# A deformable-convolution block with an expert layer: the bilinear selection weights of one lane group to a PSUM bank, built by 64-by-64 matmuls

## The reference

```python
# x + conv(ln(x)); then t + ffn(ln(t))
x_proj = inputs @ w_in + b_in
x1 = gelu(ln(depthwise3x3(inputs) + dw_bias) * gamma + beta)
offset = (x1 @ w_off + b_off)                # 8 groups x 9 taps x (x, y)
mask = softmax(x1 @ w_mask + b_mask)         # over the 9 taps of a group
px, py = pixel + tap + offset
samp = bilinear_gather(pad(x_proj), px, py)  # 8 channels of each group, 4 corners, zero outside
out = sum over taps(samp * mask) @ w_out + b_out
# ffn: 8 experts of 64 -> 256 (gelu) -> 64, the two best per token, weighted by their softmax
```

## Time and profile before

| | us |
|---|---|
| median of three runs | 310.62 |
| profiled execution | 310.67 |
| its span, first to last instruction | 308.9 |
| PE busy, of the span | 277.8 (90%) |
| ACT busy | 257.3 (83%) |
| DVE busy | 232.1 (75%) |
| POOL busy | 119.7 (39%) |

### The profile page before, as it was taken

How to read it: one execution, slowest core, us unless ns; L and a number is a source line. 1 busy time by engine, 2 the same in 40 slices (tenths; PEclk the granted TensorE clock), 3 DMA queues, 4 the chain that set the end, 5 groups by cost and what they waited for, 6 DMA issues and landing times.

```text
span 308.9 us, 8480 instructions
## 1 busy us (share of the span) xinstructions
PE 277.8 (90%) x3312; PEld 180.1 (58%) x3312; DVE 232.1 (75%) x658; ACT 257.3 (83%) x495; POOL 119.7 (39%) x123
## 2 busy tenths in 40 slices
PE   7977998968799999799999999998979999998895
PEld 2552476635468664345568664444767787676562
DVE  6999769999958859896696879599757244478455
ACT  3788679899797999998797999998868899888463
POOL 5230151504452615032194613050775903549530
PEclk9999999999999999999999999999999999999999
DMA  6920000000000000000000000000000000000000
GB/s 144 299 50 0 3 3 3 1 2 2 0 3 2 3 3 0 2 0 3 2 8 12 2 2 0 3 2 0 2 20 0 3 2 2 11 0 3 11 1 17
DMA packets 7189, 4.84 MB, mean 16 GB/s; under 512 B 5089, under 2 KB 6830, under 8 KB 7086
## 3 DMA queue, kind: packets, MB, share of 16 engines
q1 hardware_dynamic: 7150, 4.31, 5.8%
HBM read 2.04 MB, written 0.52 MB: 8 GB/s over the span
## 4 chain that ended last, share of the span: by engine, by line
PE 44%; ACT 24%; DVE 18%; issue 9%; POOL 4%; DMA 1%; DVEq 0%; ACTq 0%; POOLq 0%
ACT wk L1288 7%; ACT wk L1283 6%; PE m_ps L1653 4%; PE zl_ps L1537 4%; PE ga_ps L1568 3%; PE zh_ps L1534 3%; PE m_ps L1670 3%; PE ga_ps L1570 3%; PE ga_ps L1569 3%; ACT h_all L1319 3%; PE zl_ps L1546 2%; PE zh_ps L1546 2%; DVE prod L870 2%; PE m_ps L1682 2%; PE m_ps L1637 2%
## 5 line engine op out<-in xcount | busy, mean ns | idle before, releaser
L870 DVE TENSOR_TENSOR prod<-ga_ps,wx 128x480 f32<-128x480 f32 x96 | 62.3, 651 | 33.9 <-PE ga_ps L1570 33.6
L1283 ACT ACTIVATE wk<-zh_ps 128x512 f16<-128x512 f32 x108 | 65.2, 604 | 20.2 <-PE zh_ps L1534 19.3
L1568 PE MATMUL ga_ps<-v_all,wk 128*128 128x80 f16 x576 | 79.0, 201 | 3.0 <-DVE prod L870 1.5
L555 POOL TENSOR_TENSOR prod<-prod 128x960 f32<-128x960 f32 (+1 forms) x20 | 37.7, 1885 | 108.4 <-DVE prod L870 108.3
L1570 PE MATMUL ga_ps<-v_all,wk 128*128 128x80 f16 x576 | 79.0, 201 | 0.0
L1569 PE MATMUL ga_ps<-v_all,wk 128*128 128x80 f16 x576 | 79.0, 201 | 0.0
L1568 PEld LDWEIGHTS ga_ps<-v_all,wk 128*128 128x128 f16 x576 | 56.6, 99 | 16.2 <-issue 6.0
L1288 ACT ACTIVATE wk<-zl_ps 128x512 f16<-128x512 f32 x108 | 65.3, 605 | 0.0
L1569 PEld LDWEIGHTS ga_ps<-v_all,wk 128*128 128x128 f16 x576 | 57.1, 99 | 8.5
L1570 PEld LDWEIGHTS ga_ps<-v_all,wk 128*128 128x128 f16 x576 | 57.2, 99 | 0.0
L1537 PE MATMUL zl_ps<-tab,sel_lo 128*128 128x512 f16 x108 | 41.6, 385 | 7.2 <-ACT wk L1288 3.8
(11 more groups left out here) (284 smaller groups left out, 613.8 us busy)
## 6 DMA issues: line engine op xcount, KB each, us to landing
v_all<-still SPq DMA_DIRECT2D x1, 1440.0 KB, 10.2
h_all<-in_W SPq DMA_DIRECT2D x1, 512.0 KB
w_s<-in_W SPq DMA_DIRECT2D x1, 512.0 KB
x_tok<-in_x SPq DMA_DIRECT2D x1, 384.0 KB, 6.6
out_dram<-x_tok SPq DMA_DIRECT2D x6, 64.0 KB, 1.7
w_high<-w_high SPq DMA_DIRECT2D x1, 256.0 KB, 2.9
const<-in_table SPq DMA_DIRECT2D x1, 218.0 KB, 3.1
vec<-in_vectors SPq DMA_DIRECT2D x1, 132.5 KB
```

What stands on the lines that cost most here:

```text
L555: then(pool.tensor_tensor(p[:, 0:3, :], p[:, 0:3, :], p[:, 3:6, :], ALU.add))
L870: dve.tensor_tensor(prod[q % 2][:].rearrange("p k n -> p (k n)")[:, f * PB * NV:(f + 1) * PB * NV] .rearrange("p (n c l) -> p n c l", n=PB ...
L1283: act.activation(wk[n % WR][:, 0, :], zh_ps[:], ACT.Relu, scale=W_SCALE).then_inc(s_wkh, 1)
L1568: pe.matmul(to, w_h, high, start=True, stop=False)
```

## The change

Each of the two selection banks now belongs to one lane group g. High and low weights stand in its two partition halves: `select` multiplies the 64 table rows of lane group g by the 64 columns of `sel_hi` into the partitions of half g, and by those of `sel_lo` into the other half. A unit has four matmuls with 64 rows and 64 columns in place of two of 128 by 128, each 512 tokens wide; in the last chunk it is eight, 256 wide, of two successive taps, and the copies out of the banks have the form of the other chunks.

The image `v_all` holds four blocks of 40 columns for each pair of groups, so that one stationary slice (high and low weights of one lane group) is multiplied by two blocks: row and step, then the fp16 rest. `gather` has four matmuls of 40 columns a tile in place of three of 80, and in the last chunk it waits for both banks.

The tables, positions, masks and features are kept with the tap innermost, so `positions` and `tap_logits` take fewer, larger operations; ACT lays out the base positions once. `sel_hi` and `sel_lo` have half as many columns. The zeros of `v_all` are two DVE memsets, and the 1440 KB DMA is gone. `samples_t` of the last chunk's first half waits for the last expert activation of the chunk before. All places in the dictionaries are new (the tables of chunk four, for one, are formed after steps 35.5 and 35.5 of the third chunk in place of 33.5 and 35.5, and `half_samples_t` goes from 48.5 to 48); which instructions an engine has besides those named here is unchanged.

```diff
-NV = GC * 2 * LOC
-VW = 3 * Q * NV
+NG = GC * LOC
+NV = 2 * NG
+VW = 4 * Q * NG
+KG = P // 2
...
-FW = K2 * 2
+FW = K2
 ONE = 7 * FW
-SEL_POOL = 10
+SEL_POOL = 5
...
-        v = v_all[:].rearrange("p (b v q c g l) -> p b v q c g l", b=B, v=3, q=Q, c=GC, g=2)
+        v = v_all[:].rearrange("p (b v q n) -> p b v q n", b=B, v=4, q=Q)
...
-            sp.wait_ge(s_still, 1)
-            sp.dma_start(v_all[:, 2 * VW:].rearrange("p (n r) -> p n r", r=VW // 2),
-                         still[:, 0:VW // 2].unsqueeze(1).to_broadcast([P, 2 * (B - 2), VW // 2])).then_inc(s_vz_rest, 16)
...
-                    for t in range(2 * bank, 2 * bank + 2):
-                        dve.tensor_tensor(by_tap(py)[:, t, :, :, :], off[:, t, :, :, :, 1],
-                                          vbase[:, t % 2, :].rearrange("p (q k g) -> p q k g", q=Q, k=K2), ALU.add)
-                    for t in range(2 * bank, 2 * bank + 2):
-                        ins = dve.tensor_tensor(by_tap(px)[:, t, :, :, :], off[:, t, :, :, :, 0],
-                                                ubase.rearrange("p (q k g) -> p q k g", q=Q, k=K2), ALU.add)
+                    dve.tensor_tensor(by_tile(py)[:, t, :], off[:, t, :, 1], base_v[:], ALU.add)
+                    ins = dve.tensor_tensor(by_tile(px)[:, t, :], off[:, t, :, 0], base_u[:].unsqueeze(1).to_broadcast([P, 2, S]), ALU.add)
...
-                for t in range(TP):
-                    ins = dve.tensor_tensor(by_tap(es)[:, t, :, :, :], logit[:, t, :, :, :].rearrange("p q g k -> p q k g"),
-                                            mx[:, t, :, :].unsqueeze(2).to_broadcast([P, Q, K2, 2]), ALU.subtract)
-                ins.then_inc(s_es, 1)
+                dve.tensor_tensor(es[:].rearrange("p (t n k) -> p t n k", t=TP, k=K2), logit,
+                                  mx[:].unsqueeze(3).to_broadcast([P, TP, 2 * Q, K2]), ALU.subtract).then_inc(s_es, 1)
...
+                        ins = dve.tensor_tensor(weights[:, slots, g * LOC:(g + 1) * LOC].rearrange("p (q k t) l -> p t q k l", q=Q, t=tn),
+                                                dl[:].rearrange("p (t q g k) l -> p t q g k l", t=TP, q=Q, g=2)[:, tiles, :, g, :, :],
+                                                mask[:].rearrange("p (t q g k) -> p t q g k", t=TP, q=Q, g=2)[:, tiles, :, g, :]
+                                                .unsqueeze(4).to_broadcast([P, tn, Q, K2, LOC]), ALU.mult)
...
-                    .rearrange("p (n c l) -> p n c l", n=PB, c=GC),
-                    ga_ps[m % 2][:, 0:PB * NV].rearrange("p (n c l) -> p n c l", n=PB, c=GC),
-                    wx[j % 2][:].rearrange("p n t l -> p (n t) l")[:, m * PB:(m + 1) * PB, :]
-                    .unsqueeze(2).to_broadcast([P, PB, GC, 2 * LOC]), ALU.mult).then_inc(s_ga_rd, 1)
+                    .rearrange("p (n c l) -> p n c l", n=2 * PB, c=GC),
+                    ga_ps[m % 2][:, 0:PB * NV].rearrange("p (n c l) -> p n c l", n=2 * PB, c=GC),
+                    wx[j % 2][:].rearrange("p n t (g l) -> p (n t g) l", g=2)[:, 2 * m * PB:2 * (m + 1) * PB, :]
+                    .unsqueeze(2).to_broadcast([P, 2 * PB, GC, LOC]), ALU.mult).then_inc(s_ga_rd, 1)
...
-            dve.memset(v_all[:, 0:2 * VW].bitcast(F32), 0.0).then_inc(s_vz, 1)
-            dve.memset(feat[:, :, :, ONE:ONE + 1], 1.0)
-            dve.memset(feat[:, :, :, ONE + 1:P], 0.0)
+            pairs = v_all[:].bitcast(F32).rearrange("p (b v n) -> p b v n", b=B, v=4)
+            dve.memset(pairs[KG:P, :, 0, :], 0.0).then_inc(s_vz, 1)
+            dve.memset(pairs[0:KG, :, 3, :], 0.0).then_inc(s_vz, 1)
+            dve.memset(feat[:, :, :, ONE:P:KG], 1.0)
...
-                    act.wait_ge(s_ga, fills_done(NP * j + n - WR + 1))
+                    act.wait_ge(s_ga, fills_done(NP * j + (n - WR + 1 if j < LAST or n < WR else 2 * (n - WR + 1))))
...
-            def weights_both(n):
-
-                act.wait_ge(s_zl if n % 2 else s_zh, units_done(LAST, n // 2) + 1)
-                act.wait_ge(s_ga, fills_done(NP * LAST + n - WR + 1))
-                act.activation(wk[n % WR][:, :, tokens_of(n // NP)], z_ps[n % 2][:].rearrange("p (i n) -> p i n", i=2), ACT.Relu,
-                               scale=W_SCALE).then_inc(s_wkl if n % 2 else s_wkh, 1)
...
+            by_group = lambda t: t.rearrange("p (q k g) -> p q g k", q=Q, k=K2)
+            act.copy(base_u[:].rearrange("p (q g k) -> p q g k", q=Q, g=2), by_group(ubase))
+            for h in range(2):
+                ins = act.copy(base_v[:, h, :].rearrange("p (q g k) -> p q g k", q=Q, g=2), by_group(vbase[:, h * S:(h + 1) * S]))
+            ins.then_inc(s_base, 1)
...
+                        other = 2 * (1 - g) * QC
                         pe.matmul(to, here, own_row[:, g, :, :].rearrange("p v n -> p (v n)"), start=True, stop=False)
-                        ins = pe.matmul(to[:, 2 * QC:3 * QC], below, row_below[:, g, :], start=False, stop=True)
+                        ins = pe.matmul(to[:, other:other + QC], below, row_below[:, g, :], start=False, stop=True)
...
+            def select(g, to, n, tokens):
+
+                q, k = n // K2, n % K2
+                own, other = (slice(i * KG, (i + 1) * KG) for i in (g, 1 - g))
+                pe.matmul(z_ps[g][own, to], sel_hi[own, k, :], tokens[own, q, :], start=True, stop=True)
+                return pe.matmul(z_ps[g][other, to], sel_lo[own, k, :], tokens[own, q, :], start=True, stop=True)
+
             def weights_t(j, n):
-                q, k = n // K2, n % K2
                 pe.wait_ge(s_wkh, units_done(j, n))
-                pe.matmul(zh_ps[:], sel_hi[:, 2 * k:2 * k + 2, :].rearrange("p g m -> p (g m)"), tab[j % 2][:, q, :],
-                          start=True, stop=True).then_inc(s_zh, 1)
+                select(0, slice(0, NT), n, tab[j % 2][:]).then_inc(s_zh, 1)
                 pe.wait_ge(s_wkl, units_done(j, n))
-                pe.matmul(zl_ps[:], sel_lo[:, 2 * k:2 * k + 2, :].rearrange("p g m -> p (g m)"), tab[j % 2][:, q, :],
-                          start=True, stop=True).then_inc(s_zl, 1)
+                select(1, slice(0, NT), n, tab[j % 2][:]).then_inc(s_zl, 1)
 
             def weights_t_half(n):
 
                 half, at = n // NP, n % NP
-                q, k = at // K2, at % K2
-                pe.wait_ge(s_wkl if n % 2 else s_wkh, units_done(LAST, n // 2))
-                for part, sel in enumerate((sel_hi, sel_lo)):
-                    ins = pe.matmul(z_ps[n % 2][:, part * TH * P:(part + 1) * TH * P],
-                                    sel[:, 2 * k:2 * k + 2, :].rearrange("p g m -> p (g m)"),
-                                    tab[LAST % 2][:, q, tokens_of(half)], start=True, stop=True)
-                ins.then_inc(s_zl if n % 2 else s_zh, 1)
+                tokens = tab[LAST % 2][:, :, tokens_of(half)]
+                pe.wait_ge(s_wkh, units_done(LAST, n // 2))
+                select(0, tokens_of(0), at, tokens)
+                select(0, tokens_of(1), at + 1, tokens).then_inc(s_zh, 1)
+                pe.wait_ge(s_wkl, units_done(LAST, n // 2))
+                select(1, tokens_of(0), at, tokens)
+                select(1, tokens_of(1), at + 1, tokens).then_inc(s_zl, 1)
 
             def gather(j, n):
-                if j < LAST:
-                    pe.wait_ge(s_wkl, units_done(j, n) + 1)
-                    pe.wait_ge(s_wkh, units_done(j, n) + 1)
-                else:
-                    pe.wait_ge(s_wkl if n % 2 else s_wkh, units_done(LAST, n // 2) + 1)
+                unit = n if j < LAST else n // 2
+                pe.wait_ge(s_wkl, units_done(j, unit) + 1)
+                pe.wait_ge(s_wkh, units_done(j, unit) + 1)
                 q = (n if j < LAST else n % NP) // K2
                 tiles = range(TP) if j < LAST else tiles_of(n // NP)
                 for i, t in enumerate(tiles):
...
                     m, at = slot // PB, slot % PB
                     if at == 0 and FILLS * j + m >= 2:
                         pe.wait_ge(s_ga_rd, FILLS * j + m - 1)
-                    high, low, step = (v[:, 2 * j + t // 2, part, q, :, :, :].rearrange("p c g l -> p (c g l)")
-                                       for part in range(3))
-                    w_h, w_l = (wk[n % WR][:, part, t * P:(t + 1) * P] for part in range(2))
-                    to = ga_ps[m % 2][:, at * NV:(at + 1) * NV]
-                    pe.matmul(to, w_h, high, start=True, stop=False)
-                    pe.matmul(to, w_h, low, start=False, stop=False)
-                    ins = pe.matmul(to, w_l, step, start=False, stop=True)
+                    image = v[:, 2 * j + t // 2, :, q, :]
+                    column = i if j < LAST else n % 2 * TH + i
+                    for g in range(2):
+                        w = wk[unit % WR][:, g, column * P:(column + 1) * P]
+                        to = ga_ps[m % 2][:, at * NV + g * NG:at * NV + (g + 1) * NG]
+                        pe.matmul(to, w, image[:, 1 + g, :], start=True, stop=False)
```

(16 more changed lines are left out.)

189 lines of the change are left out of this document (92 added, 97 removed).

## The result

The changed kernel takes 320.74 us (median) against 310.62. The ratio of the comparable runs is 1.0312, 95% interval [1.0283, 1.0341]. I had forecast 316.1 us, in a range of 303 to 326, and "slower" with a chance of 0.63. So the sign and the range hold, and the forecast is 4.6 us too low.

A forecast was written before the change was run, and what follows sets the result against it. The prediction took PE and ACT, in one loop, as the bound. Terms 2.5 + 4.6 + 0.2 - 0.4 - 0.4 - 1 = +5.5 us on 310.67 gave 316.2, less 0.05 for the median: 316.1 us, range 303 to 326.

The forecast's parts named there:

- packed unit: PE, unit with both banks free: 0.90 us with four selections together, +0.04 each, +2.5 us in all.
- units that wait: PE units waiting for ACT's bank copy: 0.14 us more each, 66 of them, about half counting: +4.6 us.
- the gather: PE's sixteen 40-column gather matmuls a unit: 0.41 us against 0.43, starts about 0.0255 us apart.
- `samples_t` +0.2: Start of the last chunk: it also waits for chunk three's 16th hidden activation on ACT, +0.2 us.
- DVE -0.8: Fewer, larger DVE operations: -0.4 us at the start and -0.4 us over three chunks.
- places -1: New places for all instructions: expected to win back some of the loss, -1 us, bounds -3 and +3.
- no-overlap rival: PE's lane groups follow each other instead of overlapping: +0.29 us a packed unit, 332 us; chance 0.12.
- "shorter selection wins" rival: On PE, cheaper or hidden shape changes let the packed unit's shorter column streams decide: 304 us; chance 0.32.
- the clock: PE's granted clock was taken to stay full, as in every stretch of the profile: no cost.
- its rival: Fewer columns leave PE's array emptier and the clock falls to 1.2 GHz: about +10 us, 326; chance 0.07.

The follow-up runs named there:

- e1: The changed kernel plus 22 full-array matmuls on zeros, results unused, in the first chunk: 316.86 us, ratio 1.0178.
- e3: The changed kernel with each lane group's selection as one 128 x 128 matmul, zeros in the other group's rows, instead of small arrays: 309.78 us, ratio 0.9964.
- e5: The kernel before plus one 64 x 64 matmul of 8 columns on zeros ahead of each of 180 gathers: 330.27 us, ratio 1.0633.
- e9: The changed kernel with full-array selections, plus one 64 x 64 matmul of 8 columns on zeros ahead of each of 180 gathers: 329.81 us, ratio 1.0597.
- e8: The changed kernel with full-array selections and all places of the kernel before: 315.39 us, ratio 1.0166.
- e7: The changed kernel with all places of the kernel before: 334.78 us, ratio 1.0777.
- e11: The changed kernel with full-array selections, the last chunk's old scheme and places, and the third chunk's old places: 307.58 us, ratio 0.9890.
- e10: The changed kernel with full-array selections and the last chunk's old scheme (half unit per bank, one copy) and old places: 311.41 us, ratio 1.0017.
- e12: The changed kernel with only the third chunk's places as in the kernel before: 322.19 us, ratio 1.0310.

## Why the prediction came out as it did

The differences between versions split the change in three, beside what the prediction's own terms give for them:

| part | from | measured | predicted |
|---|---|---|---|
| small arrays, clock of chunk one kept up | e1 - e3 | +7.1 | +8.3 |
| half clock in the first chunk | changed - e1 | +3.7 | 0 |
| everything else | e3 - before | -0.8 | -2.8 |
| sum | | +10.0 | +5.5 |

What e1's fillers cost PE is in the first row and makes the second too small, by the same unknown amount.

The predicted +8.3 is the selection's share of a packed unit, 0.10 + 0.05 + 0.24 + 0.10 against 0.43, so +0.06 for 62 units counted, 3.7, and 4.6 for the units that wait. The -2.8 is the gather (-0.02 for 62), `samples_t` +0.2, DVE -0.8 and places -1.

**Right: the packed unit.** 0.025 us between gather starts (0.0255 predicted), about 0.085 and 0.12 us at the changes of shape (0.10 each), and four selections side by side, though over 0.06 us and not within 0.02. From the last gather start to the next full-array matmul, less the gather's own 0.025, it is 0.485 us, where the sum had 0.49. The no-overlap rival is out. (It had a chance of 0.12 at 332 us, above a range that was said to leave 0.09 above: the two don't fit.) The weight loads' extra 0.05 us is not separate: the way in is 0.085 us with it.

**Right in the main: the unit that waits.** ACT's wait for its selections grew from 22.7 to 31.5 us, as said, and is 22.2 in e3, while ACT's busy time moved by 1.1 us. That e1 - e3 is 7.1 against 8.3 says that the count (four fifths of 78, half of 66) was about right in sum; which of the two terms carries how much no run separates, and 13.7 us of half clock are still in e1. The "shorter selection wins" rival was to break even at 0.21 us for the way in and out together, and to win at half of 0.25. Measured are 0.205 us here and 0.19 in e5, so by that price alone a packed unit would be even; the spread of the four starts, 0.06 us for 0.02, took it back, and it is 0.485 + 0.40 = 0.885 us against 0.86.

**Wrong: the clock.** This is the step that failed. I priced it at nothing in the forecast, with 0.07 for its rival, and argued "1.00 in every stretch, under waits too". But that was so with full arrays. What PE did before the fall at 60.4 us: busy 22.91 of 24 us at the full clock, more than before the change (22.54), much of it with short columns and small arrays. e3 was busy for as long and kept the clock to 70.5 us:

```profile
36.00:60.00 24.00, 22.92 (x397) 15.97 (x396) 19.27 (x58) 19.06 (x36) 8.70 (x7) 1.00 0.02 2
```

A busy PE did not keep the clock; e1's full-array filler, on the same stretch, did. That fits the rival's mechanism ("fewer columns a unit leave the array emptier"). Neither the 40-column gathers alone (e3) nor the changes of shape (e5 and e9, with 180 pairs, have no fall before 234 us) bring such a fall. That leaves the four selections side by side; what in them does it is argued and not shown. The rival's price was too high: I had 10 us for 20 us of half clock. The median run of e1 is 3.7 us ahead of that of the changed kernel with 31 us less of it, fillers included.

**Wrong in size: the places.** The term was -1, bounds -3 and +3. The new places are worth -5.6 to the full-array version (e3 - e8) and -14.2 to the changed one (changed - e7). I reasoned that they win back "some of what is lost"; e7 shows that with the old ones the change would have cost 24 us, not 6 or 7. They are also most of why the rest came out at -0.8 and not at -2.8: the third chunk's new places make PE wait 3.25 us for `samp` (1.05 in e11); against e11 they win 1.8 us up to k = 66 and lose 5.6 behind it (e10). With e11's places and the old last chunk, "everything else" is -3.1.

**Right but small: DVE and the start.** The two position operations of the second bank start 0.22 us apart, and `es` is one operation. DVE in order of time, in the changed kernel (against the earlier trace rows):

```profile
19.73 0.31 DVE L764 TENSOR_TENSOR py<-m_ps,base_v 128x144 f32<-128x144 f32 x1
19.95 0.30 DVE L765 TENSOR_TENSOR px<-m_ps,base_u 128x144 f32<-128x144 f32 x1
...
25.95 0.46 DVE L783 TENSOR_TENSOR es<-m_ps,mx 128x288 f32<-128x288 f32 x1
```

The first multiply comes 1.0 us earlier (0.4 predicted), 0.4 in e3.

So the terms that missed are the clock (3.7) and the rest (2.0, places above all); the small arrays were over by 1.2. That gives 4.5 us against the 320.60. It is luck in part that the forecast was no further off: the miss on the small arrays went the other way, and the new places, priced at -1, measured 5.6 and 14.2 us against the old ones.

## What to carry to other kernels

By these numbers small arrays side by side pay only in longer runs than here, which no version tried: each unit paid two changes of shape, 0.19 us on PE and 0.10 on the end, to save columns that the full array streamed in 0.43 us. Keep the other half of such a change (one stationary slice for two moving blocks, fewer and larger DVE operations) and test it with the full array first: e11 is 1.1% faster than the kernel before, ratio 0.9890 [0.9865, 0.9915]. What of that is the new gather and the DVE operations, and what the new places of the first two chunks, is not shown: the kernel before was never run in new places, and with all old places the same edits (e8) are only 0.9 us ahead at k = 66 and behind at the end. And places tuned for one set of lengths can be worth more than the edit itself, so compare versions in both sets of places before an edit is judged.

## What the runs showed of the hardware

- **A busy PE can lose its clock.** With 64-by-64 selections and 40-column gathers the granted clock fell to 1.2 GHz behind a stretch in which PE was busy for 95% of the time, and stayed there for 34.1 us with PE busy for 98%. e3, which differs in the selections' shape, kept it, but for 3.5 us. Stalls go with falls too, but not one for one: where PE stood 2.8 to 3.5 us before `samples_t` (changed kernel, e1, e3, e9, e10) a fall is within 5 us, in e1 already 1.6 us before the stall; with stalls of 1.0 to 1.5 us the kernel before, e8 and e11 have none and e7 has one, at 242.3; e12, with 0.62 us, has one at 237.0. The place is not fixed either: up to the third chunk e12 is the changed kernel, and its first fall came at 69.8 us in place of 60.4.
- **Half clock costs less than half its time.** One version's runs differ in how much they have. The kernel before took 312.9 us at a mean clock of 0.989 (6.8 us of half clock) against 310.6 at 1.000: 0.34 us for each. e1's runs go from 315.5 us (0.976) to 318.27 (0.965): 2.8 for 7.1 us, 0.39; e12's from 317.79 (0.946) to 322.47 (0.917): 4.7 for 19 us, 0.25. Not all of such differences is the clock: at 1.000 the kernel before took 310.6 to 311.8 us. Changed - e1 is 0.12, with the fillers' own cost taken off. The Trainium skill, "TensorE: Matmul & The Clock Gate", section Terms, puts the penalty at the throttled time times one half, here 24 us for 47.7. No two runs of one kernel that differ by more than 5 us of half clock show that much; PE holds 64% of the chain here, not all of it.
- **Starts 0.025 us apart** with 40 columns, as with 8. The same page, section "Wait — 56ns, not 53.3ns?", says that starts are never closer than about 25 ns, however few the columns. The trace agrees.
